# Two attention stages of a 12-block decoder with other orders on their engines, and two mixtures of experts that end in scatters to DRAM and plain loads

## The chip, the cores and the metric

The program runs on one core of a Trainium2 chip. The metric is the device time of one execution in microseconds (us), from the first to the last instruction of the core; lower is better. The core has five engines with a queue each: TensorE (PE: matmuls and transposes), VectorE (DVE), ScalarE (ACT), GpSimd (POOL) and SyncE (SP, which here only issues DMAs). They meet at semaphores alone. SBUF is the on-chip memory of 128 partitions, PSUM the accumulator memory that PE writes (8 banks of 512 float32 a partition), DRAM is off chip.

## What is computed

A decoder of four layers on x of (32, 64, 128): 2048 tokens of 128 features, float32. Each of the twelve blocks adds its result to x and normalizes over the features. The two kinds of block that the change touches are the third (it holds two local attentions) and the two mixtures of experts, the sixth and the ninth.

```python
def _layernorm(x, axis=-1, eps=1e-05):
    m = jnp.mean(x, axis=axis, keepdims=True)
    v = jnp.var(x, axis=axis, keepdims=True)
    return (x - m) / jnp.sqrt(v + eps)
...
# the third block, two layers of this: 8 heads of 64, rows shifted by one token, q and k of unit length
h = shift_token(x)
q, k, v = split(h @ wqkv)
q, k = rotary_xpos(l2norm(q) * qs, l2norm(k) * ksc)
x = x + local_attention(q * 8, k, v) @ wo     # causal in a window of the 64 tokens
x = x + (a * gelu(g)) @ w2 + b2               # a, g = split(layernorm(shift_token(x)) @ w1 + b1)
...
# the sixth block (L1_MOE): every token goes to the one expert with the largest logit
y[token] = relu(x @ W1[e].T + b1[e]) @ W2[e].T + b2[e]
x = _layernorm(x + y)
...
# the ninth block (L2_MOE): the first 80 tokens of each expert only, times the probability p of the gate
y[token] = p * (gelu(x @ w1[e] + b1[e]) @ w2[e] + b2[e])   # 0 for a token beyond the 80
x = _layernorm(x + y)
```

## The kernel before

x lies in SBUF as `state`: 16 tiles of 128 tokens (two sequences of 64 each), token on the partition. The blocks run one after another as "phases", each over the 16 tiles. Two sets of buffers and PSUM banks (streams 0 and 1) take the tiles in turn; a PSUM stream has four banks. `tile_done` counts finished tiles and hands a phase to the next.

**The third block** is F0_ATTN, F0_GLU, F1_ATTN, F1_GLU. `by_tile_steps` runs them in steps: in a step each engine goes through a list written by hand (the `step` functions of `f_pool`, `f_tensor`, `f_scalar`, `f_vector`), in which `tile(n)` is the tile that entered n steps ago (lag n; tile(0) enters now). Every engine executes its list in order, so the lists alone set the order. Two steps (both streams) make one pass of the hardware loop. At the end of a phase four more steps are run that hold the last tiles of this phase and the first ones of the next, the old phase's list ahead of the new one's in each step.

What happens to one tile of F attention, with the line of the profile: POOL copies it to a staging buffer (L351); PE transposes it (L356); ACT copies it shifted (L364, L366); PE projects queries and keys (`project`, 128x512); ACT squares them (`square`, L998); DVE sums the squares and floors them (`norms`, L1039, L1042); POOL raises the 16 sums to the power -1/2 (`inverse_norms`, L905); DVE multiplies (`unit`, L1047) and makes the rotary products (`rotate`, L855 to L857); POOL adds the two halves (`rope_sum`, L910); PE transposes the heads (`turn_queries`, L825) and ACT copies them (L1002); PE makes the values (`project_values`, 128x256) and the scores (a causal table of 128x256, then 64x64 matmuls); DVE takes the maxima and subtracts (`softmax_vector`, L430, L432); ACT takes the exponential (L440); DVE sums the rows and inverts (`row_sums`, L861, L865) and divides (`normal_probs`, L886); PE transposes the probabilities (L453), ACT copies them (L447); PE mixes (64x64 matmuls), ACT copies (L1006), PE projects the output (`output`, L333 with `w_fa,arena`) and DVE adds it to the residual (`add`, L1059), which ends the tile. `headsT` and `values` share a buffer, so ACT copies the values (L1011) after the mixed heads.

**The sixth block** (`moe1_sync` ... `moe1_vector`) sorts the tokens by expert into 23 tiles of 128 rows, each of one expert (`SORTED`), in 6 groups of four (the last of three). SP stores `state` to DRAM (`moe_in`); PE, ACT and DVE find each token's expert and place; POOL gathers the rows of a sorted tile from `moe_in` by an indirect DMA (L1944). Meanwhile PE turns the one-hot choice and multiplies it by the experts' output biases, and DVE adds that to x (`m_acc`, L2180). For each sorted tile DVE copies the expert's weights (`fetch`, L2167), PE runs `up` and `down`, ACT the relu (L2073). DVE copies four finished tiles out of PSUM (`copy_out`, L2174), SP stores them to DRAM (`moe_out`). When all are stored POOL gathers them back in the order of tokens, 16 indirect DMAs (L1951), and in groups of four tiles DVE adds and takes the statistics (`group_norm_vector`, L2191, L1865 to L1873), POOL the power (L1860), and DVE writes `state` (L1877).

**The ninth block** (`moe2_*`) does the same with places 80 to an expert: 640 rows as 5 tiles of 128, L2232 for the gathers in, L2421 for the copies of turned rows, L2429 for the sums with the bias (two of 80x512), one store to `moe_out`, 16 gathers back (L2239), L2436 for the weighted sums.

After each mixture comes a phase of narrow attention, whose PE list begins so (`narrow_tensor`); `keep_busy` is matmuls whose result nobody reads:

```python
                if phases[0] in (L2_ATTN, L3_ATTN):
                    pe.wait_ge(tile_done, 2 + 16 * phases[0] - 4)
                    keep_busy(bank(1, 1) if phases[0] == L2_ATTN else bank(0, 2), 16)
                ...
                pe.wait_ge(tile_done, 2 + 16 * phases[0])
```

## Time and profile before

| | us |
|---|---|
| median of 3 runs | 1609.56 (1607.65 to 1609.67) |
| profiled execution, its own time | 1610.44 |
| its span, first to last instruction | 1608.6 |
| busy: PE, DVE, POOL, ACT | 1270.6, 1140.0, 846.8, 731.4 |
| F0 attention, first stage copy to last residual sum | 214.9 to 388.4 |
| F1 attention, last residual sum | 610.8 |
| sixth block, `state` ready to all its tiles done | 997.2 to 1110.7 |
| ninth block, the same | 1299.4 to 1371.0 |

All stages stand in a row, so the time is the sum of their lengths: the pitch of a tile (the time from one tile to the next in the steady state) times 16, and what a stage needs to fill and drain. In the rows below a duration is what one instruction took, and "idle before" is how long its engine stood still ahead of it and what ended that.

### The profile page before, as it was taken

The page shows a single profiled execution, that of the slowest core. Times are in us where ns is not written, and L with a number is a line of the kernel's source. Part 1 is how long each engine was busy: PE and PEld are TensorE (multiplying, and loading weights), DVE is VectorE, ACT ScalarE, POOL GpSimd, SP SyncE. Part 2 cuts the span into 40 slices and gives each one's busy share as a digit, 9 for nine tenths or more (in the row PEclk, how much of TensorE's full clock was granted, in tenths as well). Part 3 has the DMA queues.
Part 4 walks back from the last instruction along what each step waited for, and adds up shares of the span by engine and source line. Part 5 has one row for each costly group of instructions (what it writes and reads, how often), then busy time and mean ns, then how long its engine had stood idle before and what let it go on. Part 6 is the DMA issues. An engine that isn't in the chain of part 4 may idle for free.

```text
span 1608.6 us, 41271 instructions
## 1 busy us (share of the span) xinstructions
PE 1270.6 (79%) x15406; PEld 874.3 (54%) x15406; DVE 1140.0 (71%) x2488; ACT 731.4 (45%) x1502; POOL 846.8 (53%) x1062
## 2 busy tenths in 40 slices
PE   7988868886878867769998888883988883798871
PEld 4556636566655546546665455772555552465540
DVE  6977859983688866548886485434888843798875
ACT  3544435554555544324554354341555521455545
POOL 3543457761377644437665553426556624456654
PEclk9999989997999998879999899796999996999995
DMA  9000000000000000000000000113000013000000
GB/s 341 3 1 1 0 0 0 0 1 22 0 1 0 0 1 14 0 6 2 0 0 1 1 0 27 33 49 128 1 1 1 0 44 34 1 0 2 0 1 26
DMA packets 19559, 29.98 MB, mean 19 GB/s; under 512 B 4291, under 2 KB 16323, under 8 KB 18714
## 3 DMA queue, kind: packets, MB, share of 16 engines
q1 hardware_dynamic: 17562, 25.00, 4.5%
q0 software_dynamic: 1920, 3.94, 1.5%
q8 instruction: 51, 0.84, 0.2%
q14 instruction: 26, 0.21, 0.0%
HBM read 23.95 MB, written 4.98 MB: 18 GB/s over the span
## 4 chain that ended last, share of the span: by engine, by line
PE 38%; DVE 24%; issue 15%; POOL 13%; ACT 7%; DMA 1%; POOLq 1%; DVEq 0%; another core or an unknown queue 0%; ACTq 0%; SPq 0%
PE ps L333 31%; DVE maxima L430 6%; PE ps L453 4%; DVE arena L432 4%; ACT arena L440 3%; POOL arena L910 2%; DVE heads_out L765 2%; PE ps L825 2%; POOL arena L525 2%; POOL inv_norm L905 2%; DVE sq_sum L1039 1%; ACT arena L1231 1%; POOL arena L1951 1%; POOL rstd L371 1%; DVE gate L1806 1%
## 5 line engine op out<-in xcount | busy, mean ns | idle before, releaser
L333 PE MATMUL ps<-arena 64*64 64x64 f32 (+5 forms) x7921 | 368.4, 278 | 25.4 <-issue 5.2
L333 PEld LDWEIGHTS ps<-arena 64*64 64x64 f32 (+4 forms) x7921 | 231.4, 132 | 148.2 <-issue 112.5
L525 POOL TENSOR_TENSOR arena<-arena,w_const 128x1024 f32<-128x1024 f32 x96 | 182.4, 1901 | 151.1 <-DVE arena L755 68.0
L440 ACT ACTIVATE arena<-arena 128x1024 f32<-128x1024 f32 (+1 forms) x144 | 138.5, 962 | 111.3 <-DVE arena L432 110.5
L430 DVE TENSOR_REDUCE maxima<-ps 128x16 f32<-128x1024 f32 (+1 forms) x144 | 158.3, 1100 | 42.8 <-PE ps L333 40.7
L453 PE MATMUL ps<-w_const,arena 128*128 128x128 f32 x1024 | 142.3, 280 | 54.8 <-ACT arena L440 34.0
L905 POOL TENSOR_TENSOR inv_norm<-sq_floor,minus_half 128x16 f32<-128x16 f32 x32 | 121.9, 3810 | 84.8 <-DVE sq_floor L1042 84.6
L432 DVE TENSOR_TENSOR arena<-ps,maxima 128x1024 f32<-128x1024 f32 (+1 forms) x144 | 159.3, 1106 | 4.9
L453 PEld LDWEIGHTS ps<-w_const,arena 128*128 128x128 f32 x1024 | 114.5, 143 | 77.8 <-ACT arena L440 44.2
L371 POOL TENSOR_TENSOR rstd<-var_eps,minus_half 128x1 f32<-128x1 f32 x144 | 80.5, 570 | 132.4 <-DVE var_eps L874 89.0
L447 ACT COPY arena<-ps 128x1024 f32<-128x1024 f32 (+1 forms) x144 | 131.1, 910 | 41.5 <-PE ps L453 40.9
L765 DVE RECIPROCAL heads_out<-ps 128x128 f32<-128x128 f32 x96 | 91.4, 952 | 55.6 <-PE ps L333 55.3
L333 PE MATMUL ps<-causal,ident 128*128 128x512 bf16 (+1 forms) x305 | 83.8, 395 | 57.6 <-DVE state L1877 54.7
L333 PE MATMUL ps<-w_fa,shT 128*64 128x256 f32 (+1 forms) x384 | 104.7, 494 | 16.6 <-ACT shT L366 12.2
L689 ACT COPY arena<-ps 64x128 f32<-64x128 f32 x192 | 49.1, 256 | 102.2 <-PE ps L333 101.1
L825 PEld LDWEIGHTS ps<-w_const,arena 128*128 128x128 f32 x512 | 61.2, 149 | 56.6 <-issue 51.9
L825 PE MATMUL ps<-w_const,arena 128*128 128x128 f32 x512 | 73.1, 289 | 21.4 <-POOL arena L910 21.3
L356 PE MATMUL ps<-w_const,xs 128*128 128x128 f32 x192 | 61.7, 324 | 33.2 <-POOL xs L351 31.9
L910 POOL TENSOR_TENSOR arena<-arena 128x1024 f32<-128x1024 f32 x32 | 75.1, 2348 | 7.5 <-DVE arena L857 7.5
L356 PEld LDWEIGHTS ps<-w_const,xs 128*128 128x128 f32 x192 | 27.3, 143 | 88.0 <-issue 45.2
L1090 POOL TENSOR_TENSOR arena<-arena 128x1024 f32<-128x1024 f32 x16 | 37.7, 2358 | 68.0 <-DVE arena L857 68.0
L333 PEld LDWEIGHTS ps<-causal,ident 128*128 128x128 bf16 x305 | 26.9, 104 | 84.4 <-DVE state L1877 55.0
(320 smaller groups left out, 2671.2 us busy)
## 6 DMA issues: line engine op xcount, KB each, us to landing
experts<-in_pack_moe SPq DMA_DIRECT2D x2, 4180.0 KB, 19.9
w_fa<-in_pack_fa SPq DMA_DIRECT2D x2, 1024.0 KB, 11.8
moe_in<-state SPq DMA_DIRECT2D x2, 1024.0 KB, 5.3
w_a<-in_pack_a SPq DMA_DIRECT2D x1, 1856.0 KB, 17.0
...
ctxT<-in_ctxT SPq DMA_DIRECT2D x1, 1024.0 KB, 7.8
...
```

Of the source, the lines that this page charges most:

```text
L333: return nc.tensor.matmul(o, lhsT, rhs, start=start, stop=stop, skip_group_check=True)
L371: nc.gpsimd.tensor_tensor(rstd[s][:, :], var_eps[s][:, :], minus_half[:, 0:1], ALU.pow)\
L430: nc.vector.reduce_max(mx, sc, X_AXIS).then_inc(signal["max_ready"], 1)
L432: nc.vector.tensor_tensor(probs(s)[:, 0:heads * S].rearrange("p (a h k) -> p a h k", a=2, h=half), sc, mx.unsqueeze(3).broadcast_to([P, 2, ...
L440: nc.scalar.activation(probs(s)[:, 0:n], probs(s)[:, 0:n], ACT.Exp, scale=scale)\
L447: nc.scalar.copy(probsT(s)[:, 0:n], pair(s, 2)[:, 0:n]).then_inc(signal["probsT_ready"], 1)
L453: last = nc.tensor.transpose(pair(s, 2)[:, j * P:(j + 1) * P], probs(s)[:, j * P:(j + 1) * P], ident)
L525: nc.gpsimd.tensor_tensor(keys_wide(s).rearrange("p (b h t) -> p b h t", b=SEQS, h=8), key8(s).rearrange("p (b t) -> p b t", b=SEQS).unsqu ...
L765: nc.vector.reciprocal(heads_out[s][:, :], bank(s, 1, P, 2 * P)).then_inc(signal["sums_inverted"], 1)
L825: last = nc.tensor.transpose(pair(s, first)[:, j * P:(j + 1) * P], source[:, j * P:(j + 1) * P], ident)
L905: nc.gpsimd.tensor_tensor(inv_norm[s][:, :], sq_floor[s][:, :], minus_half[:, :], ALU.pow)\
L910: nc.gpsimd.tensor_tensor(roped(s), roped(s), rope_swapped(s), ALU.add)\
```

## The change

- **F attention, the orders.** All four lists are written anew. Projection, squares and `norms` now belong to lag 0 (they were lag 1), `inverse_norms`, `unit` and `rotate` to lag 1 (2), `rope_sum`, `turn_queries` and the copy of the queries to lag 2 (3), and the exponential and `row_sums` to lag 3 (4). Values stay at lag 2, scores at lag 3, and what follows at lag 4.
- **F attention, the division.** `normal_probs` is POOL's, at lag 4, and no longer DVE's.
- **F attention, the mixing.** For the second sequence (b = 1) the two halves of the rows are swapped in the values, the scores and the probabilities, so that the mixing matmuls of one tile take all four pairs of row half and column half, and write banks 2 and 3 in place of bank 2. The count and the shapes stay.
- **Both mixtures, the sums.** The one-hot transposes, the bias matmuls and `m_acc` of the sixth block are gone. The output bias lies beside the experts' weights, and DVE adds it to the gathered rows, sorted tile by sorted tile (`base`), then the result of four tiles (`summed`).
- **Both mixtures, the way back.** POOL scatters each sorted tile to DRAM by an indirect DMA, even tiles to one tensor and odd ones to another (`moe_back`, filled with zeros near the program's start); scatter i waits until scatter i - 2 has landed. Rows without a token go to a spare tile. SP then loads both tensors back plainly, 8 loads of 256 KB in the sixth block and 4 of 512 KB in the ninth, and DVE adds them.
- **Normalization.** In the sixth block DVE takes statistics after the loads, POOL the power and a product, and ACT writes `state`. In the ninth block the sorted rows are weighted, added to x, and normalized ahead of the scatter, two experts at a time; x itself is normalized at the start for the tokens beyond an expert's 80, and the last step is one add.
- **The ninth block's places** come straight from expert and rank: 8 gathers of 80 rows, in place of 5 of 128.
- A few semaphores are merged, and the bias bank of one narrow phase is another.

```diff
@@ f_pool
                 def step(tile):
                     for t, s in tile(0):
                         stage(t, s)
+                    for t, s in tile(4):
+                        normal_probs(nc.gpsimd, t, s, 8)
+                    for t, s in tile(1):
+                        inverse_norms(t, s)
                     for t, s in tile(2):
-                        inverse_norms(t, s)
-                    for t, s in tile(3):
                         rope_sum(t, s)
@@ f_tensor
                 def mix(t, s):
...
-                                rows, cols = slice(par * S, (par + 1) * S), slice(c * P + b * S, c * P + (b + 1) * S)
-                                last = mm(bank(s, 2)[rows, cols], values_plain(s)[rows, b, c, :],
+                                rows, cols = slice((par ^ b) * S, ((par ^ b) + 1) * S), slice(c * P + b * S, c * P + (b + 1) * S)
+                                last = mm(ps[s][par * S:(par + 1) * S, 2 + b, c * S:(c + 1) * S], values_plain(s)[rows, b, c, :],
                                           probsT(s)[rows, cols])
...
                 def step(tile):
-                    for t, s in tile(1):
-                        project(t, s)
-                    for t, s in tile(3):
-                        turn_queries(t, s)
+                    for t, s in tile(0):
+                        turn_x(t, s)
+                    for t, s in tile(4):
+                        turn_probs_pe(t, 8, streams=(s,), ready="heads_normal")
                     for t, s in tile(2):
                         project_values(t, s)
                     for t, s in tile(4):
-                        turn_probs_pe(t, 8, streams=(s,), ready="heads_normal")
+                        mix(t, s)
                     for t, s in tile(3):
                         score(t, s)
                     for t, s in tile(4):
-                        mix(t, s)
+                        output(t, s)
                     for t, s in tile(0):
-                        turn_x(t, s)
-                    for t, s in tile(4):
-                        output(t, s)
+                        project(t, s)
+                    for t, s in tile(2):
+                        turn_queries(t, s)
@@ f_vector
                 def step(tile):
-                    for t, s in tile(2):
-                        unit(t, s)
-                    for t, s in tile(4):
-                        row_sums(t, s, 8)
-                        normal_probs(nc.vector, t, s, 8)
-                    for t, s in tile(1):
-                        norms(t, s)
-                    for t, s in tile(2):
-                        rotate(t, s)
                     for t, s in tile(3):
                         softmax_vector(t, 8, streams=(s,))
                     for t, s in tile(4):
                         add(t, s)
+                    for t, s in tile(1):
+                        unit(t, s)
+                    for t, s in tile(3):
+                        row_sums(t, s, 8)
+                    for t, s in tile(0):
+                        norms(t, s)
+                    for t, s in tile(1):
+                        rotate(t, s)
@@ moe1_sync
-            for j in range(SORT_GROUPS):
-                sp.wait_ge(ms["m_copied"], j + 1)
-                sp.dma_start(sorted_rows(moe_out, j), by_tile(m_out[j % 3], j)).then_inc(stored[j % 3], 16)
+            for k in range(2):
+                sp.wait_ge(returned[k], 16 * RETURNED1[k])
+            for g in range(GROUPS):
+                for k in range(2):
+                    back(sp, 0, k, [m_gathered, m_second], 4 * g, 4 * g + 4, back_loaded[g])
@@ moe1_pool
+            def return_rows(k):
+                first, n = SETS1[k]
+                pool.wait_ge(gs["g_sum"], k + 1)
+                for i in range(first, first + n):
+                    if i >= 2:
+                        pool.wait_ge(returned[i % 2], 16 * (i // 2))
+                    nc.gpsimd.indirect_dma_start(moe_back[0][i % 2],
...
+            for j in range(2, SORT_GROUPS):
+                pool.wait_ge(ms["m_up"], 4 * j - 7)
+                fetch_rows(j)
+                if j >= 3:
+                    return_rows(j - 3)
+            for k in range(SORT_GROUPS - 3, SORT_GROUPS):
+                return_rows(k)
+            for g in range(GROUPS):
+                set_inverse(pool, g, 4 * g, 4, P)
@@ moe1_tensor
-            pe.wait_ge(ms["m_chosen"], SUMMED + GROUPS)
             turn(0)
@@ moe1_vector
             for i in range(3):
                 fetch(i)
+                base(i)
+            for i in range(3, SORTED + 3):
+                if i < SORTED:
+                    fetch(i)
+                    base(i)
+                if i % 4 == 2 and i >= 6 or i == SORTED + 2:
+                    summed((i - 3) // 4)
@@ moe2_vector, the end
+            for g in range(GROUPS):
+                dve.wait_ge(back_loaded[2 + g // 2], 32 + 16)
+                dve.wait_ge(gs["g_based"], SORTED + g + 1)
+                nc.vector.tensor_tensor(state[:, 4 * g:4 * g + 4, :].rearrange("p a n -> p (a n)"),
+                                        c_base[:, g * GT:(g + 1) * GT], c_second[:, g * GT:(g + 1) * GT],
+                                        ALU.add).then_inc(tile_done, 4)
```

How rows move. On PE, in the loop of F0 attention, stream 1's step before: `w_fa0,shT0 128x512` is the projection of the tile that entered a step ago, L825 `turn_queries`, `w_fa0,shT1 64x256` the values, L453 the turning of the probabilities, the first `arena 64x64` the scores, the second the mixing, L356 `turn_x`, `w_fa0,arena` the output.

```order
L333 MATMUL ps0<-w_fa0,shT0 128x512 x2
L285 REGISTER_ALU
L825 MATMUL ps0<-w_const,arena 128x128 x8
L254 REGISTER_ALU
L333 MATMUL ps1<-w_fa0,shT1 64x256 x4
L453 MATMUL ps1<-w_const,arena 128x128 x4
L333 MATMUL ps0<-causal16,ident16 128x256 x2
L333 MATMUL ps0<-arena 64x64 x16
L333 MATMUL ps1<-arena 64x64 x16
L254 REGISTER_ALU
L356 MATMUL ps1<-w_const,xs1 128x128
L254 REGISTER_ALU
```

The same engine and step in the changed kernel (its lines are six further down for the same helpers):

```order
L362 MATMUL ps1<-w_const,xs1 128x128
L260 REGISTER_ALU
L459 MATMUL ps1<-w_const,arena 128x128 x4
L260 REGISTER_ALU
L339 MATMUL ps1<-w_fa0,shT1 64x256 x4
L339 MATMUL ps1<-arena 64x64 x16
L339 MATMUL ps0<-causal16,ident16 128x256 x2
L339 MATMUL ps0<-arena 64x64 x16
L260 REGISTER_ALU
L339 MATMUL ps1<-w_fa0,arena 128x128 x4
L274 REGISTER_ALU
L339 MATMUL ps1<-w_fa0,shT1 128x512 x2
```

The projection moved from the head of the step to its end and is of the tile that was turned at the step's head; the mixing stands ahead of the scores.

On POOL, in the sixth block before, from the gathers in to the last power:

```order
L1944 DMA arena<-moe_in,arena 128x128 x23
L1951 DMA arena<-moe_out,arena 128x128 x8
L1860 TENSOR_TENSOR arena<-arena,minus_half 128x4
L1951 DMA arena<-moe_out,arena 128x128 x4
L1860 TENSOR_TENSOR arena<-arena,minus_half 128x4
L1951 DMA arena<-moe_out,arena 128x128 x4
L1860 TENSOR_TENSOR arena<-arena,minus_half 128x4 x2
```

And in the changed kernel, up to the first power:

```order
L1961 DMA arena<-moe_in,arena 128x128 x16
L1971 DMA moe_back<-arena 2176x128 x4
L1961 DMA arena<-moe_in,arena 128x128 x4
L1971 DMA moe_back<-arena 2176x128 x4
L1961 DMA arena<-moe_in,arena 128x128 x3
L1971 DMA moe_back<-arena 2176x128 x15
L1894 TENSOR_TENSOR arena<-arena,minus_half 128x4
```

The 16 gathers back are gone; 23 scatters stand on the same queue, 8 of them between gathers in.

## Rows read from the trace of the kernel before

**Rows 1.** The page, share of the chain that ended last, by engine:

```profile
PE 38%; DVE 24%; issue 15%; POOL 13%; ACT 7%; DMA 1%; POOLq 1%; DVEq 0%; another core or an unknown queue 0%; ACTq 0%; SPq 0%
```

**Rows 2.** Residual sums: count, ns min/median/max, first to last start; four stretches:

```profile
L1059 DVE TENSOR_TENSOR inner<-state,ps x13: 277/286/289, 247.8 to 353.0; 128x128 f32 x12, 128x128 f32<-128x128 f32 x1
L1059 DVE TENSOR_TENSOR inner<-inner,ps x13: 286/289/289, 463.2 to 576.2; 128x128 f32 x12, 128x128 f32<-128x128 f32 x1
L1059 DVE TENSOR_TENSOR inner<-state,ps x4: 286/287/288, 353.0 to 388.2; 128x128 f32<-128x128 f32 x4
L1059 DVE TENSOR_TENSOR inner<-inner,ps x4: 286/286/286, 576.2 to 610.5; 128x128 f32<-128x128 f32 x4
```

**Rows 3.** Windows: stretch, us, busy of PE, PEld, DVE, ACT, POOL; clock; DMA:

```profile
250.60:356.20 105.60, 91.46 (x1190) 63.39 (x1190) 95.09 (x146) 55.51 (x95) 79.41 (x37) 1.00 0.00 0
```

**Rows 4.** Groups by shape, 250 to 380 us: count, busy, mean ns, idle before:

```profile
L333 PE MATMUL ps<-arena 64*64 64x64 f32 x896 | 25.6, 226 | 0.0
L1047 DVE TENSOR_TENSOR arena<-ps,inv_norm 128x1024 f32<-128x1024 f32 x12 | 14.7, 1223 | 0.9
L333 PE MATMUL ps<-w_fa,shT 128*64 128x256 f32 x104 | 14.2, 392 | 0.0
L886 DVE TENSOR_TENSOR arena<-arena,inv_sum 128x512 f32<-128x512 f32 x14 | 10.0, 716 | 0.5
L432 DVE TENSOR_TENSOR arena<-ps,maxima 128x512 f32<-128x512 f32 x14 | 9.7, 692 | 0.5
L430 DVE TENSOR_REDUCE maxima<-ps 128x8 f32<-128x512 f32 x14 | 9.5, 679 | 1.6 <-PE ps L333 1.6
L861 DVE TENSOR_REDUCE row_sum<-arena 128x8 f32<-128x512 f32 x14 | 9.5, 677 | 4.3 <-ACT arena L440 4.3
L453 PE MATMUL ps<-w_const,arena 128*128 128x128 f32 x56 | 9.2, 286 | 1.9 <-DVE arena L886 1.9
L333 PE MATMUL ps<-causal,ident 128*128 128x256 bf16 x28 | 5.3, 273 | 0.0
```

**Rows 5.** One line each: POOL's division in another stage, POOL's power in F attention:

```profile
L886 POOL TENSOR_TENSOR arena<-arena,inv_sum x16: 1900/1904/1937, 711.4 to 879.2; 128x1024 f32<-128x1024 f32 x16
...
L905 POOL TENSOR_TENSOR inv_norm<-sq_floor,minus_half x32: 2915/3903/3911, 221.6 to 572.5; 128x16 f32<-128x16 f32 x32
```

**Rows 6.** Timeline, ACT, F1's last tiles: start, us, operation, idle before in brackets:

```profile
600.18 1.28 ACT L440 ACT_TABLE_LOAD   x1
```

**Rows 7.** Timeline of the sixth block, POOL, PE and DVE:

```profile
1026.33 1.12 PE L2017 MATMUL ps<-w_const,arena 128*128 128x128 f32 x4 [0.78 <-issue]
...
1039.00 0.94 POOL L1944 DMA_INDIRECT arena<-moe_in,arena  x1 [3.53 <-PE ps L333]
...
1078.01 0.56 DVE L2174 COPY arena<-ps 128x384 f32<-128x384 f32 x1 [3.68 <-PE ps L333]
...
1085.15 0.94 POOL L1951 DMA_INDIRECT arena<-moe_out,arena  x1 [0.30 <-issue]
...
1087.75 0.69 DVE L2191 TENSOR_TENSOR arena<-arena 128x512 f32<-128x512 f32 x1 [9.19 <-DMA arena<-moe_out,arena]
...
1092.20 1.26 DVE L1877 TENSOR_SCALAR state<-arena 128x128 f32<-128x128 f32 x4 [2.17 <-POOL arena L1860]
...
1109.60 1.11 DVE L1877 TENSOR_SCALAR state<-arena 128x128 f32<-128x128 f32 x4 [1.12 <-POOL arena L1860]
...
1106.21 6.22 PE L333 MATMUL ps<-causal,ident 128*128 128x512 bf16 x16 [26.78 <-DVE state L1877]
```

**Rows 8.** Timeline of the ninth block, DVE and PE:

```profile
1336.01 0.69 DVE L2429 TENSOR_TENSOR arena<-ps,arena 80x512 f32<-80x512 f32 x1 [5.73 <-PE ps L333]
...
1369.91 1.11 DVE L1877 TENSOR_SCALAR state<-arena 128x128 f32<-128x128 f32 x4 [1.12 <-POOL arena L1860]
...
1364.72 4.98 PE L333 MATMUL ps<-causal,ident 128*128 128x512 bf16 x16 [27.89 <-DVE state L1877]
```

**Rows 9.** DMA issues: what, count, KB each, median us from issue to landing:

```profile
moe_in<-state SPq DMA_DIRECT2D x2, 1024.0 KB, 5.3
```

536 lines of the change are left out of this document (292 added, 244 removed).

## The prediction

> **What bounds the kernel now.** I read the page first, then the stages the change touches, each by its own pace. The chain that ended last is spread over PE 38%, DVE 24%, POOL 13%, ACT 7% and 15% issue [rows 1]: no engine is the bound of the whole, so each stage has to be read alone, and its time adds straight to the total.
>
> In F attention the residual sums give the pace: 12 pitches from 247.8 to 353.0 are 8.77 us a tile in F0, 12 from 463.2 to 576.2 are 9.42 in F1 [rows 2]. In twelve tiles of F0 PE is busy 91.46 us, DVE 95.09, POOL 79.41 [rows 3], a tile 7.62, 7.92 and 6.62 of the 8.77. DVE is nearest, but 0.85 us a tile stands idle: the pace is set by a ring through several engines. The last three tiles of a stage are far slower, 35.2 us in F0 and 34.3 in F1 [rows 2].
>
> In the mixtures the tail matters. In the sixth block the last results leave PSUM at 1078.0 and the last tile is written at 1109.60 + 1.11 = 1110.7, so 32.7 us after the last matmul, in which DVE first waits 9.19 us for gathers [rows 7]. In the ninth it is 1336.0 to 1371.0, 35.0 us [rows 8].
>
> **F attention, the pitch.** The division leaves DVE: 0.72 us a tile [rows 4], so DVE falls to about 7.2. POOL takes it: in the next stage POOL divides 128x1024 in 1.90 us [rows 5], so half, 0.95, for 128x512, and POOL goes from 6.62 to 7.57. The mixing becomes four-quadrant matmuls. Scores and mixing together take 25.6 us in 14 tiles, 1.83 a tile [rows 4]; they have equal counts, the scores already use all four pairs, the mixing two. I estimate 0.7 for the scores and 1.15 for the mixing, and a gain of 0.5 (bounds 0, nothing runs beside anything, and 0.9, half of the pair). PE then needs 7.1. All three engines would allow 7.6.
>
> The new orders close a ring in one step: POOL's division of tile k-4 lets PE turn the probabilities, make values (k-2), mix (k-4), score (k-3); DVE then does the softmax of k-3, the residual sum, `unit` of k-1 and the row sums of k-3, which release POOL's next division. By the rows: division 0.95; turning 9.2/14 = 0.66; values 14.2/13 = 1.09; mixing and scores 1.83 - 0.5 = 1.33; causal table 5.3/14 = 0.38; maxima 0.68, subtraction 0.69; residual sum 0.29 [rows 2]; `unit` 1.22; row sums 0.68 [rows 4] and their inversion, an estimate of 0.2; three hand-overs between engines, an estimate of 0.4. Sum 8.57. Successive instructions of an engine start some 0.05 us before the shown end of the one ahead; for eight such pairs I take off 0.4: **8.2 us a tile**. ACT's copies and the exponential lie beside PE's values and DVE's `unit`. Bounds: 7.6 (POOL alone) and 8.8 (no mixing gain). So F0 saves 12 x 0.57 = 6.8 and F1 12 x 1.22 = 14.6 us. F1 runs the same lists as F0 before and is 0.65 slower a tile; I take it that the new ring settles at one pace for both.
>
> **F attention, the drain.** Before, the last tile's exponential has lag 4 and stands behind the first gelu of the next phase; ACT changes its table for it, 1.28 us [rows 6], and back. Now the exponential and the row sums of the last tile come a step earlier. What is late then is division, turning, copy, mixing, copy, output. I put the last three tiles at 8.0, 7.5 and 11 us, 26.5 in place of 35.2 and 34.3: 8 us saved in each stage, 16 in all (bounds 3 and 12 a stage). The fill holds the same chain of one tile; I cost it at nothing, within 2 us either way. F attention: **-37 us** (bounds -11 and -60).
>
> **The sixth block.** (a) PE's first transposes of sorted rows start at 1026.33 [rows 7], after the bias sums that go away. Gathers start every 0.94 + 0.30 us, and one is on chip 1087.75 - 1085.15 - 0.94 = 1.66 us after its issue ends [rows 7]; the first four are in by 1024.2. So 2.1 us are gained, less what `base` costs where it delays a weight copy; DVE has 1 us of slack a tile there. (b) POOL becomes a queue of its own weight. The gathers of the fourth group start at 1039.00 [rows 7], now at 1036.9; behind them stand 11 gathers at 1.25 and 23 scatters. A scatter may start when the one two places ahead has landed: a pair takes 0.94 + 1.66 + 0.1 = 2.7 us, 1.4 each with collisions. That ends at 1036.9 + 13.8 + 32.2 = 1082.9, landed by 1084.6, against 1075.9 for the last matmul: 8.7 us late. Bounds for a scatter: 1.25 (issue alone) and 2.0. (c) SP loads 2 MB. A 1 MB transfer in the same 512-byte rows took 5.3 us [rows 9], so 10.6. (d) After the last load DVE sums and takes statistics, POOL takes the power: before, from 1087.75 to the write at 1092.20, 4.45 us, then 1.26 [rows 7], so with the new product 5.9; since loads and sums keep pace at 2.6 a group, the end is at 8.7 + 10.6 + 5.3 = 24.6 us after the last matmul, 32.7 before. Gain 8.1. (e) PE warms up with 16 matmuls once 12 tiles are done, 6.22 us from 1106.21, ending 1.7 us after the last tile [rows 7]. The last four tiles now follow in 2.6 us, not 4.5, so that cover is gone and the next phase starts 2 us later. Sum: -2.1 - 8.1 + 2.0 = **-8 us** (bounds +8 and -13; a scatter at 2.0 adds 14).
>
> The Trainium skill, DMA: Bandwidth & Descriptors, Anatomy of one DMA, puts the fixed part of a DMA from POOL at about 2.0 us and warns of writes to DRAM; no row here has a scatter. By its figure, an estimate, a scatter costs 1.5 and the end moves 3 us.
>
> **The ninth block.** The start is about 1 us shorter in DVE's list (rows of 80, not 128) and the expert loop about 1 longer (per-expert sums, statistics, norms): nil. After the last matmul: weighting, statistics, power, norm, some 3.3 us by the pieces of the sixth block; three scatters behind them, the last landed at +8.6; the first tensor's 1 MB is loading from +7.1. Loads end 10.6 later, +17.7, and two adds of 0.7 (0.69 [rows 7]) end it at +19.1, against 35.0: 15.9 gained. The warm-up now starts 0.7 us ahead of the last tile, since groups end by single adds, and takes 4.98 [rows 8]: it ends 4.3 after, where it ended 1.3 before it. With 0.6 for copy and transpose that costs 3.7. Sum: **-12 us** (bounds -5 and -17).
>
> Semaphores merged, fills of `moe_back` at the start, larger expert loads: nil, they lie beside three blocks of work; if the fills delayed the first blocks they would cost at most their own 4 x 5.3 us [rows 9].
>
> Total -37 - 8 - 12 = -57. The profiled execution's own time is 1610.44, 0.9 above the median; 1610.4 - 57 gives **1553 us**.
>
> **Rivals.**
> 1. The ring is not shorter: the hand-overs are longer than I take them, or the mixing gains nothing, and F0 stays at 8.77 and F1 comes to it. For it: three engines at 7.1 to 7.6 leave little play. F saves 12 x 0.65 + 12 = 20, the total is 1570.
> 2. The ring is broken by slack that I don't see and POOL's 7.6 sets the pitch: 12 x (1.15 + 1.8) + 16 = 51 us, the total 1539. Against it: PE can't turn probabilities before POOL's division.
> 3. POOL's division meets DVE's `rotate`. POOL's power takes 2915 ns at its shortest and 3903 at the median [rows 5]; I read the difference as waiting for the rotary product that DVE starts beside it. The division may be held likewise, by up to this 1.0 us, in the ring: pitch 9.2, F saves 16 - 12 x 0.43 + 12 x 0.22 = 13, the total 1577. The Trainium skill, SBUF — State Buffer, Who interferes with whom, says that a DVE instruction with two SBUF inputs and a POOL instruction that reads SBUF exclude each other, whichever is first; the power's rows agree with it. I give it little, since by the lists the division runs beside `norms`, which has one input.
> 4. **Slower than before.** Scatters to DRAM land late. Each us of landing beyond 1.66 adds half a us to each of 23 + 4 scatters, about 13.5 us in all. The whole gain is gone at 1.66 + 57/13.5 = 5.9 us; at 7 us the time is 1625. Against it: SP's 1 MB store landed in 5.3 in full [rows 9].
> 5. The mixtures gain nothing (scatter at 2.0, loads slower than stores): total 1573.
>
> **Chances.** Forecast 0.56 (1540 to 1567); rival 1 0.13, rival 2 0.12, rival 3 0.06, rival 4 0.04, rival 5 0.09. Range 1533 to 1578: it leaves out rival 4 and the ends of 1, 3 and 5. A measurement here can tell 0.2%, 3 us, from no change. Faster 0.94, same 0.02, slower 0.04 (rival 4 with its neighbours).
>
> **What would show it.** Right: residual sums 8.2 us apart in both F stages, PE waiting for POOL's division at L459, one table load fewer in each drain; a scatter every 1.4 us; 24 to 25 us from the last matmul to the last tile in the sixth block, 19 in the ninth; the warm-up matmuls running past the last tile. Wrong: F0 and F1 at different pitches, the maxima not waiting for the scores, scatters 2 us apart, sorted tiles on PE waiting for rows, or a lower clock of PE where its lists were dense.

## The result, and the profile after

The changed kernel takes 1569.72 us (median of 4 runs, 1568.97 to 1570.47) against 1609.62 for the kernel before beside it: a ratio of 0.9752, 95% interval 0.9737 to 0.9768. The profiled execution has 1569.8 us of its own and a span of 1568.0, 40.6 less than before. That is inside the forecast range and 17 us short of the forecast; it is also the number that rivals 1 (1570) and 5 (1573) give, so the number alone says nothing of the reasons.

First the shares of the chain that ended last, by engine, which answers to [rows 1]. They have hardly moved:

```profile
PE 38%; DVE 24%; POOL 14%; issue 13%; ACT 7%; DMA 2%; POOLq 1%; DVEq 0%; SPq 0%; ACTq 0%
```

The residual sums of F attention after the change, cut at the same tiles as [rows 2] (count, ns min/median/max, first to last start):

```profile
L1068 DVE TENSOR_TENSOR inner<-state,ps x12: 276/277/279, 247.6 to 336.6; 128x128 f32 x12
L1068 DVE TENSOR_TENSOR inner<-inner,ps x12: 277/277/279, 455.9 to 544.9; 128x128 f32 x12
L1068 DVE TENSOR_TENSOR inner<-state,ps x4: 277/278/289, 344.7 to 375.0; 128x128 f32<-128x128 f32 x4
L1068 DVE TENSOR_TENSOR inner<-inner,ps x4: 276/277/289, 553.0 to 583.3; 128x128 f32<-128x128 f32 x4
```

From 247.6 to 344.7 are 12 pitches of 8.09 us, from 455.9 to 553.0 as well. Both stages now have one pitch, where [rows 2] had 8.77 and 9.42. The last three tiles take 30.3 us in each stage.

One step of the ring, from POOL's division of one tile to the next, in the timelines of the three engines (start, us, operation, idle before). First POOL, then PE, then DVE:

```profile
338.91 1.04 POOL L890 TENSOR_TENSOR arena<-arena,inv_sum 128x512 f32<-128x512 f32 x1 [0.28 <-DVE inv_sum L869]
...
340.01 0.66 PE L459 MATMUL ps<-w_const,arena 128*128 128x128 f32 x4 [0.17 <-POOL arena L890]
340.60 1.08 PE L339 MATMUL ps<-w_fa,shT 128*64 128x256 f32 x8
341.61 0.69 PE L339 MATMUL ps<-arena 64*64 64x64 f32 x32
342.24 0.39 PE L339 MATMUL ps<-causal,ident 128*128 128x256 bf16 x2
342.56 0.69 PE L339 MATMUL ps<-arena 64*64 64x64 f32 x32
...
343.32 0.69 DVE L436 TENSOR_REDUCE maxima<-ps 128x8 f32<-128x512 f32 x1 [0.36 <-PE ps L339]
344.05 0.69 DVE L438 TENSOR_TENSOR arena<-ps,maxima 128x512 f32<-128x512 f32 x1
344.66 0.28 DVE L1068 TENSOR_TENSOR inner<-state,ps 128x128 f32<-128x128 f32 x1
344.85 1.22 DVE L1056 TENSOR_TENSOR arena<-ps,inv_norm 128x1024 f32<-128x1024 f32 x1
345.99 0.68 DVE L865 TENSOR_REDUCE row_sum<-arena 128x8 f32<-128x512 f32 x1
346.70 0.20 DVE L869 RECIPROCAL inv_sum<-row_sum 128x8 f32<-128x8 f32 x1
```

Each row starts where the one above ends, and the next division starts at 347.02: 8.11 us after 338.91. It is the chain that the forecast wrote down. Mixing and scores are 0.69 us each: the mixing is the row ahead of the causal table, the scores the row behind it.

This step is the only one of the last seven in which the division waits for DVE. In the others POOL's own queue is as late, or later. The middle of F0, POOL and then DVE:

```profile
312.13 2.35 POOL L914 TENSOR_TENSOR arena<-arena 128x1024 f32<-128x1024 f32 x1
...
314.67 1.04 POOL L890 TENSOR_TENSOR arena<-arena,inv_sum 128x512 f32<-128x512 f32 x1
...
314.34 0.20 DVE L869 RECIPROCAL inv_sum<-row_sum 128x8 f32<-128x8 f32 x1
```

The sums are inverted at 314.54, and the division starts at 314.67, when POOL has done its rotary sum and a stage copy. So a second chain is as long as the forecast's within 0.1 us a tile. It takes two steps: from a division through PE's mixing, scores and projection to ACT's squares, DVE's `norms`, POOL's power (3.8 to 3.9 us) and rotary sum (2.35), and on to the division after the next (298.50 to 314.67). A shorter first chain alone would gain almost nothing. This is read from the timelines, no run takes the two apart.

The 40.6 us by stretches. "Forecast" is the prediction's own term, "measured" the difference of the two traces:

| stretch | forecast | measured |
|---|---|---|
| up to the first residual sum of F0 (start -1.7, fill +1.6) | 0 | -0.1 |
| F0, 12 pitches | -6.8 | -8.2 |
| F0, last three tiles (35.2 to 30.3) | -8 | -4.9 |
| last sum of F0 to first sum of F1 (75.1 to 80.9) | 0 | **+5.9** |
| F1, 12 pitches | -14.6 | -15.9 |
| F1, last three tiles (34.3 to 30.3) | -8 | -4.0 |
| to the store of the sixth block (386.7 to 384.1) | 0 | -2.7 |
| sixth block, store to first turned rows (29.2 to 26.8) | -2.1 | -2.4 |
| sixth block, first turned rows to last sum (51.7 to 57.4) | 0 | **+5.7** |
| sixth block, last sum to last tile (32.7 to 23.6) | -8.1 | -9.1 |
| narrow phase behind it (188.7 to 192.0) | +2.0 | +3.3 |
| ninth block, store to first turned rows (20.7 to 20.1) | -1 | -0.6 |
| ninth block, expert loop (15.9 to 20.2) | +1 | **+4.4** |
| ninth block, last matmul to last tile (35.0 to 19.3) | -15.9 | -15.8 |
| the rest (214.7 to 218.3) | +3.7 | +3.7 |

Three stretches that were costed at nothing or at 1 us took 16 us. The drains (the last three tiles of a stage) gave 7 less than forecast. The steady part gave 3 more.

**From F0_GLU to F1.** PE in the steps that hold the GLU's last tiles and F1's first (timeline, as above):

```profile
415.50 1.95 PE L339 MATMUL ps<-w_fa,shT 128*128 128x512 f32 x4 [0.76 <-ACT shT L372]
...
420.89 1.05 PE L339 MATMUL ps<-w_fg,arena 128*128 128x128 f32 x6 [2.11 <-DVE arena L1477]
...
422.92 3.75 PE L339 MATMUL ps<-w_fa,shT 128*128 128x512 f32 x4 [0.77 <-ACT shT L372]
432.47 1.62 PE L339 MATMUL ps<-w_fg,arena 128*128 128x128 f32 x6 [5.80 <-DVE arena L1477]
```

and the windows of two of these stretches (us, busy PE, PEld, DVE, ACT, POOL; PE's granted clock; DMA share, GB/s):

```profile
414.00:422.00 8.00, 5.13 (x30) 3.52 (x28) 2.45 (x6) 3.14 (x9) 1.94 (x1) 0.97 0.00 0
422.00:428.00 6.00, 3.90 (x5) 1.18 (x4) 1.75 (x3) 1.54 (x3) 1.63 (x3) 0.50 0.00 0
```

PE waits 2.11 and 5.80 us for DVE's GLU product (L1477), which in DVE's joint steps stands behind `norms` of the tile that has just entered F1, and so behind its turning, copying, projection and squaring. The second wait stands behind `rotate` of the tile before as well. Before, `norms` had lag 1, so only the last GLU tile stood behind a wait of DVE for squares (3.33 us, at 435.03). After the wait of 2.11 the projection takes 3.75 us and not 1.95: the granted clock is 0.50, the 1.2 GHz level. The GLU's last sums are at 412.1, 414.7, 422.0 and 434.2; before they were 2 to 3 us apart but for the last, which came 7 later. The clock is not the same in every execution: in e9_warm_longer, whose code is the same here, the wait of 2.11 comes too, but the projection behind it takes 1.95 us:

```profile
420.85 1.95 PE L339 MATMUL ps<-w_fa,shT 128*128 128x512 f32 x4 [0.77 <-ACT shT L372]
```

There the crossing from F0 to F1 takes 77.6 us. In the five other profiles with this code it takes 80.9 to 82.8.

**The sixth block.** PE, the turning of sorted rows:

```profile
1016.16 0.60 PE L2032 MATMUL ps<-w_const,arena 128*128 128x128 f32 x4
...
1025.73 0.66 PE L2032 MATMUL ps<-w_const,arena 128*128 128x128 f32 x4 [1.82 <-DMA arena<-moe_in,arena]
...
1036.67 0.90 PE L2032 MATMUL ps<-w_const,arena 128*128 128x128 f32 x3 [3.14 <-DMA arena<-moe_in,arena]
1037.37 12.55 PE L339 MATMUL ps<-arena 128*128 128x128 f32 x88
```

and POOL. The first row is the first gather of the fifth group, behind four scatters that start 1.4 to 1.8 us apart; the second is one of the sixth group, behind four more:

```profile
1018.92 0.99 POOL L1961 DMA_INDIRECT arena<-moe_in,arena  x1 [0.30 <-PE ps L339]
...
1031.16 1.36 POOL L1961 DMA_INDIRECT arena<-moe_in,arena  x1 [0.30 <-issue]
...
1055.07 0.97 POOL L1971 DMA_INDIRECT moe_back<-arena  x1 [0.30 <-issue]
1056.34 0.97 POOL L1971 DMA_INDIRECT moe_back<-arena  x1 [0.30 <-DMA moe_back<-arena]
```

PE stands still for rows that POOL had not fetched yet, and its clock falls (88 matmuls in 12.55 us; in the steady part 64 take 7.31). The tail is nearly as forecast: scatters 1.27 apart where none has to wait for one ahead of it, 1.35 on average over the last seven, the first sum of loaded rows at 1062.49, the last tile at 1075.0.

**The ninth block.** Windows of the expert loop, before the change and then, in two parts, after it:

```profile
1320.10:1336.00 15.90, 15.39 (x136) 14.69 (x134) 2.15 (x6) 7.84 (x32) 2.08 (x3) 1.00 0.06 14
```

```profile
1287.00:1296.00 9.00, 8.19 (x44) 8.04 (x45) 1.51 (x6) 2.65 (x12) 5.19 (x6) 0.62 0.12 32
1296.00:1307.40 11.40, 10.91 (x97) 10.28 (x95) 7.02 (x34) 6.67 (x26) 5.18 (x8) 1.00 0.05 13
```

Before, the 14 warm-up matmuls ran straight into the first rows. Now they end 1.3 us ahead of them, and PE's granted clock averages 0.62 over the first 9 us of the loop.

### The profile page after: what moved, and what is told of

It reads as the page before. It is cut to its first block, busy times and chain, and to the rows that moved or that the text cites. A ratio compares the mean times of both kernels' runs of the same rounds, so it can differ in the third digit from the quotient of the medians.

```text
span 1568.0 us, 41351 instructions
## 1 busy us (share of the span) xinstructions
PE 1256.6 (80%) x15361; PEld 853.4 (54%) x15361; DVE 1120.7 (71%) x2495; ACT 734.9 (47%) x1529; POOL 883.2 (56%) x1106
## 4 chain that ended last, share of the span: by engine, by line
PE 38%; DVE 24%; POOL 14%; issue 13%; ACT 7%; DMA 2%; POOLq 1%; DVEq 0%; SPq 0%; ACTq 0%
PE ps L339 31%; DVE maxima L436 6%; PE ps L459 4%; DVE arena L438 4%; POOL inv_norm L909 3%; ACT arena L446 3%; DVE heads_out L769 3%; POOL arena L914 2%; POOL arena L531 2%; PE ps L829 2%; DVE sq_sum L1048 1%; ACT arena L1005 1%; ACT arena L1239 1%; DVE gate L1815 1%; POOL rstd L377 1%
## 5 line engine op out<-in xcount | busy, mean ns | idle before, releaser
L339 PE MATMUL ps<-arena 64*64 64x64 f32 (+5 forms) x7921 | 359.8, 281 | 23.8 <-ACT arena L453 8.3
L339 PEld LDWEIGHTS ps<-arena 64*64 64x64 f32 (+4 forms) x7921 | 218.9, 134 | 156.8 <-issue 125.6
L459 PE MATMUL ps<-w_const,arena 128*128 128x128 f32 x1024 | 143.3, 282 | 41.0 <-ACT arena L446 33.8
L459 PEld LDWEIGHTS ps<-w_const,arena 128*128 128x128 f32 x1024 | 115.7, 144 | 58.0 <-ACT arena L446 44.0
L453 ACT COPY arena<-ps 128x1024 f32<-128x1024 f32 (+1 forms) x144 | 131.2, 911 | 19.0 <-PE ps L459 18.5
L829 PE MATMUL ps<-w_const,arena 128*128 128x128 f32 x512 | 74.1, 292 | 31.4 <-POOL arena L914 30.3
L829 PEld LDWEIGHTS ps<-w_const,arena 128*128 128x128 f32 x512 | 61.5, 151 | 68.3 <-issue 66.0
L890 POOL TENSOR_TENSOR arena<-arena,inv_sum 128x512 f32<-128x512 f32 (+1 forms) x48 | 65.7, 1369 | 34.8 <-DVE inv_sum L869 34.6
```

The lines of the kernel that those rows point to most:

```text
L339: return nc.tensor.matmul(o, lhsT, rhs, start=start, stop=stop, skip_group_check=True)
L453: nc.scalar.copy(probsT(s)[:, 0:n], pair(s, 2)[:, 0:n]).then_inc(signal["probsT_ready"], 1)
L459: last = nc.tensor.transpose(pair(s, 2)[:, j * P:(j + 1) * P], probs(s)[:, j * P:(j + 1) * P], ident)
L829: last = nc.tensor.transpose(pair(s, first)[:, j * P:(j + 1) * P], source[:, j * P:(j + 1) * P], ident)
```

## Experiments

The runs were made in three groups, each on one chip, beside the kernel before on that chip (1608.84, 1612.20 and 1613.45 us). Which chip the changed kernel's own profile above is from is not on record; its stretches are like those of the first group (e1 to e4). Ratios are to the kernel before on the same chip, with 95% intervals; where a stretch decides, it is read from the trace of the run.

### 1. The two halves of the change, and two repairs

`e1_f_only` takes F attention's four lists from the changed kernel into the kernel before, `e2_moe_only` the other way round.

> The kernel before with F attention's part of the change alone (orders, division on POOL, four-quadrant mixing). Theory A: the parts add, and each is worth what the two traces show for its stretch of the program. By the residual sums F attention ends 27.2 us earlier (610.48 to 583.25), and 2.7 more are gained up to the store of the sixth block; so 1609.6 - 29.9 = 1580 (1578 to 1582), and the mixtures keep their 113.5 and 71.6 us. Rival: the forecast's 37 us for F are there, and part of them is lost only because the mixtures of the changed kernel run at another clock; then 1573.

> The changed kernel with the four lists of F attention of the kernel before: the mixtures' part alone. Theory A: 1569.7 + 29.9 = 1599.6 (1597 to 1602): the sixth block is 5.7 shorter, the narrow phase behind it 3.2 longer, the ninth 11.9 shorter, the last stretch 3.7 longer. Rival: the 2.7 us between F attention's end and the sixth block belong to the bank of the narrow phases and the packs, not to F attention; then 1597. Rival as in the run ahead: 1590.

Measured: 1578.78 (0.9815, 0.9796 to 0.9835) and 1598.22 (0.9929, 0.9903 to 0.9954). They take 30.1 and 10.6 us off, 40.7 together, and the whole change took 39.9. The parts add; theory A holds, and F attention is not held back by the mixtures. In `e1_f_only` F attention ends at 582.2. From there to the store it takes 386.1 us, in the other profiles of this study 383.9 to 388.3, so the 2.7 us of that row of the table are within what differs from one execution to the next.

```diff
 # e3_gathers_first
-            for j in range(2):
-                fetch_rows(j)
-            for j in range(2, SORT_GROUPS):
-                pool.wait_ge(ms["m_up"], 4 * j - 7)
-                fetch_rows(j)
-                if j >= 3:
-                    return_rows(j - 3)
-            for k in range(SORT_GROUPS - 3, SORT_GROUPS):
-                return_rows(k)
+            for j in range(SORT_GROUPS):
+                fetch_rows(j)
+            for k in range(SORT_GROUPS):
+                return_rows(k)
```

> The changed kernel with all 23 gathers of the sixth block issued ahead of the first scatter, and without the waits on PE's progress between them. Theory B: in the changed kernel PE waits for sorted rows because gathers of groups 4 to 6 stand behind scatters on POOL's queue; from the first turned tile to the last sum it takes 57.4 us where it took 51.7. With the gathers first (issued by 987.5 + 23 x 1.25 = 1016) PE's waits for rows are gone, the loop takes 52, the tail stays at 23.6, and the time falls by 5.5 to 1564. Rival: the scatters, which now start at 1016 instead of 1012.6, end later than the last sum plus three, and the tail takes back what the loop gives: 1568 to 1571. Second rival: PE is slow there because its clock is low; then the loop stays at 57 and the time at 1569.7.

Measured: 1564.40 (0.9713, 0.9686 to 0.9740). The loop takes 50.8 us in place of 57.4, the tail 26.3 in place of 23.6. PE, the turns of groups 5 and 6:

```profile
1025.14 0.60 PE L2027 MATMUL ps<-w_const,arena 128*128 128x128 f32 x4
...
1032.73 0.49 PE L2027 MATMUL ps<-w_const,arena 128*128 128x128 f32 x3
```

Neither waits. On this chip the queue order was the cause of the 5.7 us, theory B: the other profiles of this chip with the old queue order (e2, e4) have loops of 57.7 and 56.4 us. Of the 6.5 that the loop gains the tail takes 2.7 back, which the theory had not expected and its first rival had.

```diff
 # e4_glu_first, in by_tile_steps
-                for j in range(back):
+                gap = 1 if (last_ph, ph) == (F0_GLU, F1_ATTN) else 0
+                for j in range(back + gap):
                     for n in STREAMS:
                         if last_step:
                             last_step(tiles_at(whole(last_ph, TURNS + j), n))
-                        if step:
-                            step(tiles_at(whole(ph, j), n))
+                        if step and j >= gap:
+                            step(tiles_at(whole(ph, j - gap), n))
```

> The changed kernel with F1_ATTN's first steps put off by one pass of the loop (two steps) behind F0_GLU, on all engines; nothing else. Theory C: the last three tiles of the GLU are slow (sums at 412.1, 414.7, 422.0, 434.2 where they were 2.7 apart) because in every joint step the GLU's product on VectorE stands behind projection, squares and norms of the tile that enters F1, and in the old lists it did not. Then the last GLU sum comes at about 420, 14 us earlier, and the first residual sum of F1, a fill of 34 us behind the first copy at about 420, at 454 where it is at 455.9: 1568 (1565 to 1570). Rival: the joint steps are slow for F1's own chain and the low clock; then the GLU's end gains nothing that F1 sees, and putting off two steps costs their full length less the overlap: 1574 to 1578.

Measured: 1566.82 (0.9733, 0.9717 to 0.9749). The GLU's last sums are 2.2 us apart, and the last comes at 418.4 in place of 434.2:

```profile
416.18 0.29 DVE L1488 TENSOR_TENSOR inner<-gate,ps 128x128 f32<-128x128 f32 x1 [1.16 <-PE ps L340]
418.40 0.29 DVE L1488 TENSOR_TENSOR inner<-gate,ps 128x128 f32<-128x128 f32 x1 [1.16 <-PE ps L340]
```

So theory C holds for the GLU's tail: it was F1's list that held it. The crossing takes 77.2 in place of 80.9, but e9 has 77.6 without this edit and e10 79.4 with it, and the interval of the ratio overlaps that of the changed kernel. The 3 us of gain fit the theory and are not shown clear of noise. In the crossing that is left PE again runs a projection in 3.78 us.

### 2. What sets F's pitch

`e5_mix_two_pairs` is the changed kernel with the old layout of values, scores and mixing; `e6_division_dve` moves `normal_probs` to VectorE behind `row_sums`; `e7_mix_only` is the kernel before with the new mixing (the diff lines of `mix`, `project_values`, `score` and the copy of the heads, and nothing else); `e12_table_once` is the kernel before with one more instruction:

```diff
 # e6_division_dve, in f_pool and f_vector
-                    for t, s in tile(4):
-                        normal_probs(nc.gpsimd, t, s, 8)
                     for t, s in tile(3):
                         row_sums(t, s, 8)
+                        normal_probs(nc.vector, t, s, 8)
 # e12_table_once, in by_tile_steps
                 if step:
+                    if ph == F1_ATTN and eng is scalar_engine:
+                        nc.scalar.activation(warm[:, :], warm[:, :], ACT.Exp)
                     with eng.Fori(0, TURNS - back) as turn:
```

> The changed kernel with values, scores, probabilities and mixing laid out as before, so that the mixing uses two pairs of row half and column half and writes one bank. Theory D: the mixing lies in the ring that sets the pitch. In the changed kernel scores and mixing take 0.69 us each, before they took 1.77 together, so the mixing should take 1.08 again, 0.39 more; the pitch of the residual sums goes from 8.09 to 8.48 in both stages, 2 x 16 x 0.39 = 12 us: 1582 (1578 to 1584). Rival: PE has play (it waits 0.8 to 0.9 us a tile for POOL's rotary sum ahead of turn_queries), so the longer mixing eats that play and the pitch stays at 8.1 to 8.2: 1570 to 1573.

> The changed kernel with the division of the probabilities on VectorE, right behind the row sums, and not on POOL. Theory D (the forecast's): a ring of PE, DVE and POOL sets the pitch. The division takes 0.70 in place of 1.04, and the hand-over to POOL goes away, but it now stands on DVE, which is busy 7.3 us of 8.09 a tile, ahead of norms and rotate: DVE is busy 8.0 and cannot be idle less than the 0.6 it waits for squares and scores, so the pitch is 8.4 to 8.7 and the time 1580 to 1590. Rival: PE's wait for POOL's chain (power, rotary sum, then the division) is what holds the ring; with POOL at 6.6 instead of 7.7 the pitch stays at 8.1 or falls, and the time is 1566 to 1571.

> The kernel before with the four-quadrant mixing alone: old orders, division on VectorE. Theory: mixing takes 0.39 us less a tile on PE. In the old orders DVE's residual sum waits for PE's output, 6.6 us in 12 tiles of F1, and F0's ring goes through the mixing too; if the whole 0.39 counts, 32 tiles give 12 us: 1597. Rival: in the old orders the pitch hangs on DVE, POOL and PE by another way, DVE has 7.9 of 8.77 busy, and the mixing is worth at most a third: 1605 to 1609.

> The kernel before with one more instruction: ahead of F1's loop, on ScalarE, an exponential of one column that nobody reads. In the kernel before F1's loop holds a table load of 1.28 us at the head of each pass (six of them), F0's holds none. Theory G: that is the whole difference of the two pitches, 9.41 against 8.77: 1.28 us a pass of two tiles is 0.64 a tile. With the table loaded once ahead of the loop, F1's pitch is 8.77, 12 x 0.64 = 7.7 us less: 1601.5 (1600 to 1603). Rival: F1 is slower because it reads and writes the same tensor or starts from another phase; ACT has 4 us a tile to spare and hides the load, the pitch stays at 9.4 and the time at 1609.

| kernel | us, ratio (95%) | pitch F0 | pitch F1 |
|---|---|---|---|
| before (F0 without any edit is 8.67 to 8.77 in three profiles) | | 8.77 | 9.41 |
| e7: new mixing alone | 1603.50, 0.9949 (0.9926 to 0.9971) | 8.56 | 9.22 |
| e12: table loaded once | 1603.65, 0.9940 (0.9924 to 0.9957) | 8.68 | 8.81 |
| e5: new orders, POOL's division, old mixing | 1593.23, 0.9887 (0.9861 to 0.9912) | 8.53 | 8.53 |
| e6: new orders, new mixing, DVE's division | 1581.12, 0.9799 (0.9755 to 0.9843) | 8.27 | 8.31 |
| changed | 1569.72, 0.9752 (0.9737 to 0.9768) | 8.09 | 8.09 |

**Mixing.** In the old layout PE shows 1.15 us for mixing and 0.69 for scores, in the new one 0.69 for both: 0.46 less, the forecast's estimate of 0.5. In the new ring the pitch pays 0.44 of it (e5 against changed), in the old orders 0.1 to 0.2 (e7 against before). The whole of e7 gained 8.7 us, between its two expectations; 5 of them are the pitches. Theory D holds for the pitch. The rival's play is not there: what PE idles ahead of `turn_queries` doesn't absorb a longer mixing. Both chains above hold the mixing, so e5 doesn't tell them apart. The total of e5 is further off (21.7 us by the ratios, 12 expected); 10.6 of it are the 24 pitches, part of the rest is a sixth block of 113.4 us (below).

**Division.** On DVE the pitch is 0.2 longer, between the two expectations. DVE then works back to back, and hardly waits any more:

```profile
313.20 0.79 DVE L890 TENSOR_TENSOR arena<-arena,inv_sum 128x512 f32<-128x512 f32 x1
...
317.82 0.69 DVE L436 TENSOR_REDUCE maxima<-ps 128x8 f32<-128x512 f32 x1
```

DVE is busy 95.4 of 99.3 us in these twelve tiles, and 87.7 of 97.1 in the changed kernel. It is bound by DVE, not by the ring. So, within the new orders, moving the division to POOL is worth 0.2 us a tile, and only because DVE was then full.

**The table.** The kernel before holds this group in F1, 463 to 576 us (count, busy, mean ns, idle before); in the steady part of F0, and of both stages of the changed kernel, there is no such row:

```profile
L364 ACT ACT_TABLE_LOAD x5 | 6.4, 1283 | 0.1
```

It stands at the head of the hardware loop: the exponential with lag 4 first runs inside the loop, the table that is loaded when the loop is entered is the GLU's, so the load was put into the loop's body and runs in each of its six passes of two tiles. With one exponential ahead of the loop F1's pitch falls from 9.41 to 8.81, so the loads are nearly the whole difference of the two stages: theory G. The rule of 1.28 / 2 = 0.64 a tile fits only by chance: the 12 pitches hold five loads, not six, and they cost 7.2 us (112.9 to 105.7), 1.4 each. The whole kernel gained 9.8 us, 8.1 expected. In the new orders the exponential has lag 3, so its first one runs in the step ahead of the loop, and the load with it. The Trainium skill, ScalarE: Activation LUTs, What ACT_TABLE_LOAD costs, gives a drain of about 1.38 us on top of the 1.28 of the load, 2.66 for a switch to another set. Five of them would be 13.3 us, an estimate; the trace shows 7.2. Nor is there a drain ahead of a load: in F1's last tiles ACT ends its gelu at 600.16 and the load starts at 600.18 [rows 6].

### 3. Warm-ups

```diff
 # e8_warm_early, ahead of the narrow phases
-                    pe.wait_ge(tile_done, 2 + 16 * phases[0] - 4)
+                    if phases[0] == L2_ATTN:
+                        pe.wait_ge(tile_done, 2 + 16 * phases[0] - 8)
+                    else:
+                        pe.wait_ge(back_loaded[2], 32 + 16)
 # e9_warm_longer, ahead of the ninth block's expert loop
-            keep_busy(bank(1, 0), 14)
+            keep_busy(bank(1, 0), 20)
```

`e10_all_four` has e3, e4, e8 and e9 together; `e11_after_again` is the changed kernel, on the chip of e9 and e10.

> The changed kernel with the warm-up matmuls ahead of the two narrow phases started earlier: behind the sixth block after 8 of its tiles instead of 12, behind the ninth when SP's last loads have landed and not when 12 tiles are written. Theory E: the warm-up's end, not the last tile, starts the next phase (1078.46 against 1075.1, 1331.2 against 1326.7). Then the next phases start 1.8 and 4.0 us earlier, 5.8 in all: 1564. Rival: the 16 matmuls are there to raise the clock; behind an earlier warm-up PE idles again and its clock falls, as it does at 1084 to 1090 in the changed kernel, and what is gained is given back at half speed: 1567 to 1571.

> The changed kernel with 20 in place of 14 warm-up matmuls ahead of the ninth block's expert loop. Theory F: the loop takes 20.2 us where it took 15.9 because PE runs it at half clock up to 1295.5 (8 matmuls of 128x128 in 1.91 us, not 1.04): the rows now come 1.3 us after the last warm-up matmul, where they used to be there before its end. Six more at 0.227 us fill the gap, the loop takes 16 to 16.5 and the time falls by 4: 1565.7 (1564 to 1567.5). Rival: the loop is slow by its hand-overs (each expert's product must be read out by VectorE before the next but one is written, and ACT has gelu and norms); then the loop stays at 19 to 20 and the time at 1569 to 1570.

> The changed kernel with four edits together: all gathers ahead of the scatters (as in the run e3_gathers_first), F1 two steps later (e4_glu_first), the warm-ups earlier (e8_warm_early), and 20 warm-up matmuls ahead of the ninth block's loop (e9_warm_longer). Each repairs another stretch, so they should add: 5.3 + 2.9 + 6.1 (by its two stretches) + 4 = 18 less than the changed kernel: 1551 (1547 to 1556), 0.965 of the kernel before. Rival: the edits share the clock and the queue, and a third of it is lost: 1557 to 1562.

> The changed kernel itself once more, beside the other three on the same chip, as their base. 1569.7 as before; where a chip's sixth block is slower for all kernels with scatters (113 to 115 us in place of 108, as in the runs e5 to e8) it shows here too, with 1574 to 1576.

Measured: e8 1571.02 (0.9763, 0.9726 to 0.9801), e9 1576.65 (0.9783, 0.9753 to 0.9812), e10 1574.83 (0.9773, 0.9749 to 0.9798), e11 1573.97 (0.9748, 0.9719 to 0.9778). The first three were expected at 1564, 1565.7 and 1551; none of them is faster than the changed kernel. By stretches of the profiled executions (us; that of e11 is its slowest of five, 1579.2):

| kernel | sixth: loop, tail | narrow phase | ninth: loop | rest |
|---|---|---|---|---|
| changed | 57.4, 23.6 | 192.0 | 20.2 | 218.3 |
| e8 | 63.2, 23.3 | 188.9 | 20.4 | 216.0 |
| e9 | 64.7, 23.4 | 193.4 | 23.3 | 218.2 |
| e10 | 70.1, 23.0 | 188.5 | 23.2 | 215.5 |
| e11 | 65.6, 23.3 | 191.9 | 20.4 | 217.9 |

**Earlier warm-ups** (e8, e10) do shorten what they touch: the narrow phase by 3, the rest by 2.3 to 2.8. Theory E holds for its two stretches; the total doesn't show it, since the sixth block's loop is longer on this chip (below). In the changed kernel the clock falls once more behind the warm-up, in e8 it does not. First the window of the changed kernel, then that of e8:

```profile
1083.50:1090.50 7.00, 6.87 (x33) 2.49 (x34) 4.16 (x4) 2.17 (x6) 1.28 (x3) 0.51 0.57 244
```

```profile
1086.00:1094.00 8.00, 6.45 (x52) 3.36 (x50) 5.45 (x6) 3.92 (x9) 2.93 (x4) 1.00 0.71 306
```

**The longer warm-up** (e9, e10) fails on this chip. PE starts the ninth block's loop at full clock (8 matmuls in 1.06 us, not 1.91). But then DVE and ACT stand still for 5.8 and 3.4 us, with a releaser that the profile doesn't know (it writes "remote"), PE waits for DVE, and runs at half clock from 1299.6 to about 1305. The rows of e9, and last the same wait of DVE in e11:

```profile
1298.73 0.29 DVE L2485 TENSOR_TENSOR arena<-ps,experts 80x128 f32<-80x128 f32 x1 [5.76 <-remote]
...
1298.86 0.98 ACT L2378 ACTIVATE arena<-ps,experts 128x80 f32<-128x80 f32 x4 [3.39 <-remote]
...
1299.61 1.99 PE L339 MATMUL ps<-arena,experts 128*128 128x80 f32 x8 [2.92 <-DVE arena L2478]
...
1304.39 0.29 DVE L2485 TENSOR_TENSOR arena<-ps,experts 80x128 f32<-80x128 f32 x1 [5.68 <-remote]
```

The loop gets 3 us longer. In both kernels DVE goes on 8.5 us after PE's first turned rows (1290.19 and 1295.88), whatever PE's clock. All six kernels with scatters on the two later chips have this wait of DVE, 5.0 to 5.9 us, and none on the first chip. So the half of theory F on the clock is right. Whether a longer warm-up gains where this wait is absent, no run shows.

**The sixth block on other chips.** On the second and third chip its loop takes 63 to 70 us in all six kernels with scatters (e5, e6, e8 to e11), the changed kernel itself among them; with the old mixtures (e7, e12) it is 51, as before. The waits of DVE and ACT there (engine, line, releaser: us, times, longest), first the changed kernel as e11, then e10 with all gathers in front:

```profile
DVE arena L2189 <- remote: 6.7, 3, 3.2
ACT arena L2085 <- remote: 5.4, 3, 4.0
```

```profile
DVE arena L2188 <- remote: 22.5, 2, 13.5
ACT arena L2084 <- remote: 18.8, 2, 16.3
```

DVE, ACT and PE stand still together, while POOL issues indirect DMAs back to back (in e10 up to 1011.5; DVE is held from 991.5 to 1004.9 and from 1005.9 to 1014.9). On the first chip e3, with the same order, has none of these waits. So the repair of e3 gains 5 us on one chip, and on another the loop that holds it (e10) is 4.5 us longer than the changed kernel's own (e11). No repair here is shown to gain on more than one chip. What holds the three engines is open: the profile names no semaphore for it, and in e10 no packet of the instruction queues starts between 990.3 and 1024.7, so the stall doesn't end with one.

## Why the forecast came out 17 us too large

- **The pitch**: right, mechanism and size. 8.2 forecast, 8.09 measured, the ring as written, both stages alike. The step "the new ring settles at one pace for both" was an assumption; the reason is the table load in F1's loop, of the kind in [rows 6], which the prediction did not look for. It made the F1 term right by luck: some 0.6 of its 1.33 us a tile is the table, not the ring. That POOL's own chain is as long as the ring, the prediction did not see either: it gave POOL its busy time of 7.6 as the bound. Rival 1 is excluded (pitch 8.09, not 8.77), rival 2 too (POOL busy 7.3 to 7.4 us a tile, the pitch above it).
- **The drain**: the mis-sized term. 26.5 forecast, 30.3 measured in both stages. The step that failed is "the last three tiles at 8.0, 7.5 and 11". They take 13.1, 7.6 and 9.6. In the first one PE waits 2.63 us for POOL's rotary sum and then runs at half clock. In PE's joint step the turning of the probabilities (L459) then stands behind the turning of the GLU's entering tile (L1375). That waits for ACT's shifted copy, which stands behind the copy of the queries. The timelines of the changed kernel, PE, POOL, DVE:

```profile
346.97 1.94 PE L829 MATMUL ps<-w_const,arena 128*128 128x128 f32 x8 [2.63 <-POOL arena L914]
...
350.44 0.48 PE L1375 MATMUL ps<-w_const,shT 128*128 128x128 f32 x1 [1.31 <-ACT shT L372]
350.71 1.06 PE L459 MATMUL ps<-w_const,arena 128*128 128x128 f32 x4
...
347.02 2.02 POOL L890 TENSOR_TENSOR arena<-arena,inv_sum 128x512 f32<-128x512 f32 x1
...
348.06 1.53 DVE L860 TENSOR_TENSOR arena<-arena,rope_f 128x512 f32<-128x512 f32 x1
```

  In steady state L829 takes 1.06, the division (L890) 1.04 and L860 0.71, and from L829 to the turning (L459) it is 1.2 us, here 3.7. In e3_gathers_first F0's drain took 28.0, with that tile at 11.2, L829 at 1.06 and 2.9 up to L459, so the clock is some 2 of the 3.8 us; the wait for the GLU's tile is about the rest. The size also differs from one execution to the next: 27.9 to 30.3 in the eight profiles with the changed F attention, 34.3 to 36.9 with the old lists (before, e2, F0 of e12). The -4.9 and -4.0 of the table are near the low end of what the drains give. The gelu's table load still stands ahead of the last tile's copy (368.27, then the copy at 370.32); one load went, as forecast.
- **Rival 3** has its mechanism here, at no cost. In the drain no tile enters, so DVE has no `norms` to do, `rotate` starts at once and meets the division: both take about double. The division still ends at 349.04, 1.7 us before PE turns its result at 350.71. In steady state they never meet, as the prediction argued. The Trainium skill, SBUF — State Buffer, Who interferes with whom, lets a DVE instruction with two SBUF inputs and a POOL instruction that reads SBUF exclude each other; the 2.02 and 1.53 us agree.
- **The fill costed at nothing**: "within 2 us either way" held for F0 (+1.6) and failed for F1 (+5.9), since F1's fill runs in joint steps with the GLU's tail. The lag-0 chain was looked at for its own tile and not for the queue behind it. e4 shows this for the GLU's tail. Some 3 us of the 5.9 hang on the clock: e9's crossing is 77.6, 2.6 above before, with the projection at full clock.
- **The sixth block**: start and tail right (-2.4 and -9.1 for -2.1 and -8.1). The tail's sum has a slip: it adds 5.3 behind the loads where the sentence has 5.9. The step "POOL becomes a queue of its own weight" followed the scatters behind the gathers and not the gathers behind the scatters; "sorted tiles on PE waiting for rows" stood in the list of signs only. On the first chip e3 shows it: 57.4 to 50.8 us.
- **Scatters**: 1.27 to 1.3 us apart where the queue is free, landing 2.3 us after the start of their issue at the median. Rivals 4 and 5 are excluded: the mixtures gain 10.6 us alone (e2).
- **The ninth block**: tail 19.3 for 19.1. "The expert loop about 1 longer" was a count of work and left out the clock: 4.4.
- **Warm-ups**: cost 3.3 and 3.7 for 2.0 and 3.7, as described; the extra 1.3 fits the second fall of the clock, which is absent in e8.
